# Part of the W_O product of tile 0 moved into the last attention step, and the loads of the merge stage split over two queues

## What is computed

```python
x = x + _L0_xattn_ref(_layernorm(x), mask, ctx_2048, ctx_2048, wq, wk, wv, wo)      # cross attention, 256 keys
x = x + _L0_attn_ref(_layernorm(x), W_Q, b_Q, W_K, b_K, W_V, b_V, W_O, b_O)         # 16 heads of 128, rotary, causal
x = x + _L0_ffn_ref(_layernorm(x), gate_up_packed, gate_up_scales, down_packed, down_scales)

# inside the second:  z = einsum('bnqk,bknd->bqnd', probs, V)
#                     out = einsum('bqnd,ndm->bqm', z, W_O) + b_O
# inside the third:   the weights are 4-bit codes, 8 in an int32, with a scale per 128 inputs;
#                     h = silu(gate) * up;  y = h @ w_down.T;  y / sqrt(mean(y*y) + 1e-6)
```

## Time and profile before

| | us |
|---|---|
| median of three runs (1486.67 to 1486.99) | 1486.83 |
| the profiled execution, whole | 1487.69 |
| its span, first to last instruction | 1485.9 |
| TensorE busy | 1381.2 |
| VectorE busy | 979.9 |
| ScalarE busy | 512.7 |
| GpSimd busy | 446.0 |
| merge stage, from its first matmul to the barrier behind it | 987.53 to 1178.06 |

### The profile page before, as it was taken

The page is one execution under the profiler, slowest core; times in us unless marked ns, Lnnn a source line. Parts: engine busy times, 40 slices in busy tenths (PEclk is TensorE's granted clock), DMA queues, the critical chain, the costliest instruction groups (busy, mean ns, idle before and its releaser), DMA issues. The chain is left out here.

```text
span 1485.9 us, 25221 instructions
## 1 busy us (share of the span) xinstructions
PE 1381.2 (93%) x8788; PEld 808.1 (54%) x8788; DVE 979.9 (66%) x2187; ACT 512.7 (35%) x1221; POOL 446.0 (30%) x306
## 2 busy tenths in 40 slices
PE   8999999868899989998999999977899899999997
PEld 6666666434566656665666666643344434343433
DVE  6443443457777687777777777725929796969693
ACT  3222223222333333333333343320001383838281
POOL 0000000004333243333333343305001292929292
PEclk9999999989999999999999999979899899999999
DMA  8555555240100110002000000067642000000000
GB/s 319 210 207 209 211 185 198 100 154 23 39 28 28 57 56 28 24 19 85 28 28 28 15 29 28 28 222 183 188 112 97 1 1 22 7 21 7 22 7 29
DMA packets 59504, 122.01 MB, mean 82 GB/s; under 512 B 4280, under 2 KB 37816, under 8 KB 52792
## 3 DMA queue, kind: packets, MB, share of 16 engines
q1 hardware_dynamic: 59448, 121.27, 23.7%
HBM read 96.09 MB, written 25.17 MB: 82 GB/s over the span
## 5 line engine op out<-in xcount | busy, mean ns | idle before, releaser
L854 POOL TENSOR_TENSOR hd_rotated<-hd_products 64x512 f32<-64x512 f32 x64 | 112.8, 1763 | 718.6 <-DVE hd_products L1039 718.6
L183 PE MATMUL psum<-hd_xt_hi,hqk_hi 128*128 128x512 f16 x512 | 198.1, 387 | 4.9 <-DVE hd_xt_lo L1009 4.9
L184 PE MATMUL psum<-hd_xt_lo,hqk_hi 128*128 128x512 f16 x512 | 197.5, 386 | 0.0
L185 PE MATMUL psum<-hd_xt_hi,hqk_lo 128*128 128x512 f16 x512 | 196.8, 384 | 0.0
L1355 POOL TENSOR_TENSOR ff_part<-ff_part 128x512 f32<-128x512 f32 x88 | 127.6, 1465 | 100.2 <-DVE ff_part L1482 99.9
L183 PE MATMUL psum<-hd_wv_hi,hd_xt_hi 128*128 (+1 forms) x512 | 140.3, 274 | 5.3 <-DVE hd_wv_lo L1014 5.3
L1384 PE MATMUL psum<-ff_xt_hi,gu 128*128 128x512 f16 x352 | 135.1, 384 | 8.3 <-DVE ff_part L1482 3.3
L184 PE MATMUL psum<-hd_wv_lo,hd_xt_hi 128*128 (+1 forms) x512 | 140.2, 274 | 0.0
L185 PE MATMUL psum<-hd_wv_hi,hd_xt_lo 128*128 (+1 forms) x512 | 140.2, 274 | 0.0
L1385 PE MATMUL psum<-ff_xt_lo,gu 128*128 128x512 f16 x352 | 134.4, 382 | 0.0
L1482 DVE SCALAR_TENSOR_TENSOR ff_part<-psum,gu_scale,ff_part 128x512 f32<-128x512 f32 x176 | 119.8, 738 | 8.3 <-PE psum L1385 4.2
(11 more groups left out here) (165 smaller groups left out, 2826.4 us busy)
## 6 DMA issues: line engine op xcount, KB each, us to landing
xa_kv_t<-in_ctx_t_dram SPq DMA_DIRECT2D x16, 1024.0 KB, 4.8
xa_kv<-in_ctx_dram SPq DMA_DIRECT2D x16, 1024.0 KB, 4.8
w_rows<-in_head_weights_dram SPq DMA_DIRECT2D x12, 1024.0 KB, 6.9
z_scratch<-hd_z_hi SPq DMA_DIRECT2D x32, 256.0 KB, 2.2
z_scratch<-hd_z_lo SPq DMA_DIRECT2D x32, 256.0 KB, 2.3
w_rows<-z_scratch SPq DMA_DIRECT2D x8, 1024.0 KB, 7.8
mg_codes<-_ffn_gate_up_packed_dram SPq DMA_DIRECT2D x4, 1408.0 KB
xn<-in_x_dram SPq DMA_DIRECT2D x8, 512.0 KB, 3.6
```

Source lines behind the costliest of these rows:

```text
L183: pe.matmul(out, lh, rh, start=(first and i == 0), stop=False)
L184: pe.matmul(out, lh, rl, start=False, stop=False)
L185: last = pe.matmul(out, ll, rh, start=False, stop=(final and i == k - 1))
L854: pool.tensor_tensor(rotated[0:HALF, w, 0, :], products[0:HALF, w, 0, :], products[0:HALF, w, 2, :], ALU.subtract)
```

## The change: what it does

Four things.

1. Half 0 of tile 0 (96 matmuls, heads 0 to 7) leaves the merge stage. It goes into the last attention step in four blocks of 24: one behind the scores, one behind the transposes, two behind the product with v. The last step uses other PSUM banks (a section `"last"`), and tile 0 of the merge stage banks 4 to 7. SP loads the first half of z one tile earlier in its program, behind the first pair of the last tile, and TensorE waits for it in the last step.
2. SP's last attention step loads ahead what the merge stage starts with, once the last projection of k is done and the q and k weights are free: half 1 of tile 0, x1 of tile 0 alone, b_O, shift, scales and codes 0. They land in the space of `hqk_hi` and `hqk_lo` (`Early`).
3. In the merge stage codes 1, the 15 issues for the down matrix, codes 2 and codes 3 are issued by ScalarE. SP's program has z and x1 alone. GpSimd adds b_O to the four blocks of tile 0 at once and to the other 12 when x1 of tiles 1 to 3 has landed.
4. In the FFN stage x2, `h_hi`, `h_lo` and `result` lie in space that was used before; no instruction of that stage changes.

```diff
 HEADS_SMALL = 6
+MERGE_BANKS = (4, 0)
+def merge_heads(pe, out, z, wo_hi, wo_lo, half, at):
+    z_hi, z_lo = z
+    n = HEADS // 2
+    for i in range(n):
+        head = half * n + i
+        pe.matmul(out, z_hi[:, i, at], wo_hi[:, head, :], start=(head == 0), stop=False)
+        pe.matmul(out, z_hi[:, i, at], wo_lo[:, head, :], start=False, stop=False)
+        last = pe.matmul(out, z_lo[:, i, at], wo_hi[:, head, :], start=False, stop=(head == HEADS - 1))
+    return last
...
@@ heads_phase, SP
+                if last_tile:
+                    load_first_z()
...
-                sp.wait_ge(small_loaded_z_stored, 16 * (HEADS_SMALL + 2 * (NT - 1) * PAIRS))
+                sp.wait_ge(small_loaded_z_stored, 16 * (HEADS_SMALL + 2 * ((NT - 1) * PAIRS + 1)))
...
+            def load_for_merge(last_proj):
+                banks.wait_filled(sp, last_proj, ("k", 1))
+                for half in range(2):
+                    sp.dma_start(early.second_z[half], z_of(z_scratch, half, 1, 0)).then_inc(early_sems.z_loaded, 16)
+                sp.dma_start(early.x2[:, 0:TT, :], rows_of(0)).then_inc(early_sems.x1_loaded, 16)
+                sp.dma_start(early.b_o, b_o.broadcast_to([P, D])).then_inc(early_sems.b_loaded, 16)
+                sp.dma_start(early.shift, shifts).then_inc(early_sems.small_loaded, 16)
+                sp.dma_start(early.gu_scale_f16, gu_scales).then_inc(early_sems.small_loaded, 16)
+                sp.dma_start(early.codes, codes_of(gu_codes, 0)).then_inc(early_sems.codes_loaded, 16)
...
                 if not s.proj:
-                    load_first_z()
+                    load_for_merge({"turn": NT, "proj": s.a})
...
-            sp.wait_ge(first_z_loaded, 32)
@@ heads_phase, TensorE
+            def merge_first(s, i):
+                banks.wait_room(pe, s.runs_z, ("merge", i))
+                merge_heads(pe, psum_of(("merge", i)), first_z, wo_hi, wo_lo, 0, slice(i * P, (i + 1) * P))
...
+                else:
+                    pe.wait_ge(first_z_loaded, 32)
+                    merge_first(s, 0)
                 if s.att:
                     pe.wait_ge(probs_ready, s.a + 1)
...
+                else:
+                    merge_first(s, 1)
...
+                if not s.proj:
+                    merge_first(s, 2)
+                    merge_first(s, 3)
@@ merge_phase, SP
-            load_z(0, 1)
-            sp.dma_start(x2[:, :, :], x1_rows.rearrange("(b p) d -> p b d", p=P)).then_inc(x1_loaded, 16)
...
+            load_z(1, 0)
+            load_x1(1)
+            sp.wait_ge(z_used[1], 1)
+            load_z(1, 1)
+            for t in range(2, NT):
+                load_x1(t)
+            for t in range(2, NT):
...
                 for half in range(2):
-                    sp.wait_ge(z_used[half], t)
+                    sp.wait_ge(z_used[half], t - 1 + half)
                     load_z(t, half)
-                if t <= 2:
-                    sp.wait_ge(gu_decoded, t)
-                    load_codes(t + 1)
@@ merge_phase, ScalarE
+            load_codes(1)
+            act.dma_start(down_c[:, 0, :], down_codes[0:WHOLE, :]).then_inc(down_loaded, 16)
...
+            for g in range(2, KD):
+                act.wait_ge(gu_decoded, g - 1)
+                load_codes(g)
```

More of the change, by code:

```diff
@@ L696, with __init__, take, codes_of @@
 HEADS_SMALL = 6
+MERGE_BANKS = (4, 0)
+class Early:
+    def __init__(self, hqk_hi, hqk_lo):
+        flat = hqk_lo[:, :, :].rearrange("p a n -> p (a n)")
+        at = [0]
+        def take(n):
+            at[0] += n
+            return flat[:, at[0] - n:at[0]]
+        half = HEADS // 2
+        self.x2 = hqk_hi[:, :, :].rearrange("p a n -> p (a n)").bitcast(F32).rearrange("p (b d) -> p b d", d=D)
+        self.second_z = tuple(take(half * TILE).rearrange("p (h t) -> p h t", t=TILE) for _ in range(2))
+        self.b_o = take(2 * D).bitcast(F32)
+        self.codes = take(2 * GU).bitcast(I32)
+        self.gu_scale_f16 = take(KD * 2 * FB)
+        self.shift = take(2).bitcast(I32)
+class EarlySems:
+    def __init__(self, nc, ctx):
+        self.z_loaded = ctx.enter_context(nc.semaphore("early_z_loaded"))
+        self.x1_loaded = ctx.enter_context(nc.semaphore("early_x1_loaded"))
+        self.b_loaded = ctx.enter_context(nc.semaphore("early_b_loaded"))
+        self.small_loaded = ctx.enter_context(nc.semaphore("early_small_loaded"))
+        self.codes_loaded = ctx.enter_context(nc.semaphore("early_codes_loaded"))
+def codes_of(gu_codes, g):
+    words = gu_codes[WORDS * g:WORDS * (g + 1), :]
+    return words.unsqueeze(0).broadcast_to([8, WORDS, GU])
+def merge_heads(pe, out, z, wo_hi, wo_lo, half, at):
[7 more added lines that the diff above has]
+    return last
 def z_of(z_scratch, hi_or_lo, half, t):
@@ L754, in heads_phase @@
             "att": [("scores", 4), ("probs", 5), (("z", 0), 0), (("z", 1), 1)],
+            "last": [("last_scores", 2), ("last_probs", 3), (("last_z", 0), 0), (("last_z", 1), 1)] +
+                    [(("merge", i), MERGE_BANKS[0] + i) for i in range(TT)],
         })
@@ L780, in __init__ @@
                 self.runs_z = {"turn": self.turns_now, "proj": g + 1 if proj else g, "att": a}
+                self.scores, self.probs, self.z = "scores", "probs", "z"
+                if not proj:
+                    self.runs_scores = self.runs_z
+                    self.scores, self.probs, self.z = "last_scores", "last_probs", "last_z"
         def for_each_step(eng, on_the_side, step):
@@ L1565 @@
+        flat = hqk_lo[:, :, :].rearrange("p a n -> p (a n)")
+        h_hi, h_lo = (flat[:, i * FB * TILE:(i + 1) * FB * TILE].rearrange("p (b t) -> p b t", t=TILE) for i in range(2))
+        result = w_rows[:, 0, :].rearrange("p (b d) -> p b d", d=D)
+        ffn_phase(nc, psum, ident, early.x2, xn, stat, gu, gu_scale, down_hi, down_lo, h_hi, h_lo, result, out.rearrange("b s d -> (b s) d"))
 _INS = ["x", "ctx_2048", "ctx_t", "L0_xattn_wq", "L0_xattn_wk", "L0_xattn_wv", "L0_xattn_wo",
```

154 lines of the change are left out of this document (74 added, 80 removed).

## The result

The changed kernel takes 1476.28 us (median of four runs, 1474.54 to 1477.32), the kernel before 1486.8 beside it: a ratio of 0.9923, 95% interval 0.9909 to 0.9937. It is faster, but by 10.5 us and not by the 36.8 forecast, and the time lies outside the range of 1446 to 1458. The profiled execution took 1477.32, its span is 1475.5 (before 1485.9).

What follows compares the result with a forecast made beforehand. The prediction saw TensorE as the bound, idle in the last attention step, at a late z load and before the FFN stage; 13.7 + 17.3 + 3.8 + 2.0 = 36.8 us less gave 1450.0 us, range 1446 to 1458.

Steps and rivals of the forecast that it cites:

- The half in the last step: Last attention step: half 0 woven in starts half 1 of tile 0 13.7 us earlier, at 997.0; bounds 12.7 to 14.1.
- The rival in which the blocks sit on the softmax's chain: Last attention step: block one ends behind the softmax and delays it; 1451, rival four, included in the sum's 0.74.
- The wait of 15.3 us: Merge stage: TensorE's wait for the first half of z of tile 1 goes; 17.3 us less.
- The stretch forecast at 145.1 us: Merge stage: TensorE runs seven halves without a stop, from 997.0 to 1142.1.
- the second: Merge stage: z and codes share the engines, so TensorE still waits at 1017.7; 1467 us, chance 0.09.
- The third: Merge stage: interleaved queues starve z in the first three loads, making the kernel slower; 1502 us, chance 0.02.
- The rule of the Trainium skill that the prediction cited: SP's and ScalarE's transfers interleave on the same 16 DMA engines; a second queue saves only issue time, so z lands later.
- Slower by the queue split: Merge stage: the third rival's claim that interleaved queues starve z and make the kernel slower; 1502 us, chance 0.02.
- The end of the merge stage: Merge to FFN stage: VectorE ends 0.7 us behind TensorE, gap 1.1 instead of 5.0; 3.8 us less, 0 if VectorE stays late.
- VectorE did not become the bound: Merge stage, rival one: VectorE, slowed beside GpSimd and waiting for codes, ends behind TensorE; 1455 or so, chance 0.15.
- The start of the FFN stage: First FFN transposes and matmuls: the clock may stay at the higher level after shorter idle; 2.0 us less, between 0 and 3.9.
- every term of the prediction at its high end: Whole kernel: gains of 14.1, 17.3, 3.8 and 3.9 us together give 1447.7 us.

Runs made afterwards that it cites:

- b: Changed kernel with each load of codes cut into 11 loads of 256 columns (1 KB rows), same queues: 1447.57 us, then 1448.10 us in five more executions.
- g: Kernel before with only codes and down loads moved to ScalarE's queue, in 11 KB rows, nothing done early: 1494.11 us.
- h: Changed kernel with codes 1 to 3 and the down loads back on SyncE in the old order, early half and early loads kept: 1467.77 us.
- a: Changed kernel with codes 1 to 3 and down matrix loads back in SP's one queue, ordered by need, codes 1 behind z(1,0): 1448.43 us.
- j: Kernel before with only FFN weight loads moved to ScalarE's queue, each load of codes cut into eleven with 1 KB rows: 1466.48 us.

## Why the prediction was wrong

**The half in the last step: right.** Forecast 13.7 us earlier, with half 1 of tile 0 at 997.0; it came at 995.79, 14.95 earlier. 0.68 of that lies ahead of the step (scores at 970.95 against 971.63). The other 14.27 are 0.57 more than forecast and just beyond the upper bound of 14.1: by the distances of starts the transposes took 0.49 instead of 0.60, the product with v 1.79 instead of 1.95, the barrier 0.45 instead of 0.7. The rival in which the blocks sit on the softmax's chain is out: from scores' end to transposes passed 5.42 us, before 5.42 too.

**The wait of 15.3 us: wrong, and it is the step that failed.** I took 16.0, the slowest landing of the earlier trace rows, as the bound for z beside the codes. Those rows were of loads that shared one queue with the codes, each behind or ahead of them; none showed a z load against 11 KB packets in a second queue. In the changed kernel z(1,0) arrived 33.4 us after its issue. The stretch forecast at 145.1 us took 174.4; of the 29.3 too much 12.44 and 11.42 are the waits, and of the remaining 5.4 the half clock behind them makes 5.1 (PEclk 0.50 in the windows above): 15 matmuls from 1029.12 took 6.04 us instead of 3.24, 12 from 1064.23 took 4.92 instead of 2.59. Behind the one wait of before it was 1.8. The term of -17.3 became +12.0. b shows that the term itself was sound: without the crawl the seven halves take 145.0.

I also read the DMA engines' busy share of 0.52 with 119 GB/s in the earlier trace rows as room. I now take it for the codes keeping half of the engines busy: from 1049 to 1055, with work in both queues, the shares add up to 51% again. The other half is then no room for a z load that is spread over all of them and is complete only with its slowest piece, which would also be why SP's queue moved 1.59 MB in the first 10 us and 0.36 in the next 11. This reading is argued from shares and counts; no run tests it apart.

**The rivals.** The mechanism was there, in the second and third, with 0.09 and 0.02. The third wanted each of three loads 12.3 us late, 2 MB in over 33 us. Two of three were about that late (12.44 and 11.42), and took 33.4 and 47.5 us from issue to use, and the third was not waited for: from 1064 to 1068 the engines moved 342 GB/s again (windows above). I held the 313 GB/s and the 16.0 against it, which were rates of one queue. The rule of the Trainium skill that the prediction cited was on the right side: z landed later, in up to 44.7 us instead of 16.0.

**Slower by the queue split: true of that part.** g says that the part that I gave 17.3 us costs 6.6 by itself (0.26 to 0.55%); h that the early half with its loads is worth 19.8. Their sum, -13, is near the measured -10.5.

**The end of the merge stage: right**, 3.75 for 3.8. VectorE did not become the bound; idle before the first transpose was 1.05 as forecast. The changed kernel alone tests that weakly, since its last matmul came 28 us later than forecast and left VectorE that much more time; but in b, where it came at 1140.14, the idle is 1.05 too. VectorE waited up to 4.6 us for codes, more than the 2 that the prediction allowed, at no cost. The runs g and h show that the quick end comes from the early issue of codes 2 and 3.

**The start of the FFN stage: 3.7 instead of 2.0**, near the upper bound of 3.9: the transposes took 1.94 instead of 3.65, and the stage 304.1 us.

Put together with b: 1447.7 was the time with every term of the prediction at its high end, and with packets of 1 KB the kernel takes 1448.1. a and b, which can't be told apart (1448.43 and 1448.10), beat both kernels, by 2.6% against the one before and by 1.9% against the one after.

## What to carry to other kernels

Before giving a load a queue of its own, compare the lengths of the rows in both queues: if engines serve the queues packet for packet, as here row for row, the queue with the short rows gets the short end (0.07 MB against 0.73 here). Cut the long rows to the length of the urgent load's, or keep one queue and put the urgent load first; both took all the waits away in the changed kernel (in j, with the order of before, 3.10 us were left). And a landing time from a trace bounds a landing only while the same neighbours share the engines.

## What the runs showed of the hardware

- A change of the rows' length in another engine's loads alone, 11 KB to 1 KB, moved the landing of 1 MB from 24.7 to 9.9 us, and the kernel by 28 us; smaller packets lost nothing that shows here (233 GB/s at a share of 0.80 from 1000 to 1020 in b):

```profile
1000.00:1020.00 20.00, 20.00 (x95) 9.05 (x93) 17.01 (x37) 0.00 (x0) 1.99 (x2) 1.00 0.80 233
```

- One issue can hold its engine for long, and with it all that stands behind it in the program: SP was held at the load of b_O (256 KB, behind x1 of 4 MB) for 7.72 us in the kernel before, 16.49 in j and 47.40 in g.
- Behind 1.05 us of idle ahead of the FFN stage the granted clock stayed at the higher level (1.00 from 1171.3 to 1176 in after) and 16 transposes took 1.94 us (after, b, g, j). Behind 5.02 us it was at the lower (0.50 from 1160 to 1164 in h) and they took 3.65, as behind 4.81 before.
